# Pacing the gathers of GpSimd by their own landings: a graph attention and mixture-of-experts kernel

## Chip, cores and metric

The kernel runs on one core of one Trainium2 chip. The metric is device time in microseconds (us) of one execution; the median of the runs is compared. The profile comes from one further execution of the same program.

## The reference

3,125 nodes with 256 features and 50,000 edges, sorted by their target node. The input is normalised, a graph attention layer (8 heads of 32) and a second branch ("mix") are added to it, and then a layer of 8 weighted experts.

```python
xn = _layernorm(x, axis=-1)
# graph attention
h_prime = (xn @ W + b).reshape(n, K, F_OUT)
h_src = jnp.sum(h_prime * a_src, axis=2); h_trg = jnp.sum(h_prime * a_trg, axis=2)
e = leaky_relu(h_src[src] + h_trg[trg], 0.2)
exp_e = jnp.exp(e - jnp.max(e))
alpha = exp_e / (segment_sum(exp_e, trg)[trg] + 1e-10)
gnn = segment_sum(h_prime[src] * alpha[:, :, None], trg)
# mix: q, k, v of xn by a batch-normalised product, depthwise and grouped
# products, relu attention within a node, a residual product
x = x + gnn + mix(xn)
# experts: softmax weights w, two batch-normalised relu layers, output product
x = x + sum_e w[:, e] * (relu(bn(relu(bn(xn2 @ W1[e])) @ W2[e])) @ Wo[e] + bo[e])
```

## The kernel before

**Stages.** Up to about 67 us the nodes are projected, and a table `projected_rows` with 264 floats a node (256 projected features and 8 source scores) is written to device memory. Then come the edges, until about 670 us. The experts (feed-forward part) fill the rest.

**The edges.** They are cut into NG = 33 groups of EC = 12 chunks of 128 edges (the last group has 7 chunks). For a group `grp` these things are done, each engine running its own loop over the groups and all of them held together by semaphores:

- GpSimd, `gather(grp)` (L431 to L447): one indirect DMA for each chunk (L444) fetches the 128 rows of the sources from the table into `G[slot][:, c, :]`. There are SLOTS = 5 buffers G. It runs ahead of the other engines by LEAD = 2 groups.
- SyncE, `targets(g)` (L360): loads the targets of a group, spread over all partitions, into `dstb`, 384 KB, two buffers.
- VectorE, `window(g)`: makes a one-hot matrix `ohT` from `dstb` and the scores of the targets' window, `hsel`.
- TensorE, `targets(g)` (L757, raises `hte_ready`): twelve small matmuls of `ohT` and `hsel`, the target score of every edge.
- VectorE, `scores(g)` (L1175 on): waits for the gathers of g and for `hte_ready`, and adds source and target scores. ScalarE takes the exponentials (L489, L493).
- VectorE, `messages(g)`: a one-hot matrix `oh` (L1206), then the rows in G times the exponentials (L1218).
- TensorE, `sums(g)` (L768, raises `seg_ready`): twelve matmuls of `oh` and G, 128 x 264, which add the messages up by target.
- VectorE, `collect(g)` (L1224): adds the sums to the accumulator and raises `g_free` (L1257), so that the buffer G may be filled again.

**The mix branch** is woven into the same loops, one node tile (128 nodes, NT = 25) an iteration, t = g - 2: TensorE's `channels` (L803), `u_rows` (L814, three matmul pairs, each raising `u_mm`), `out_features` (L821) and `mixed_out` (L828, the residual product, raises `r_mm`); ScalarE's `squares` (L504, L506), `epsilon` and `mixed_out` (L527, which waits for `r_mm`); VectorE's `mix(t)` (L1320 to L1328).

**Order within an iteration g.** TensorE: targets(g+1), out_features, u_rows, early channels, sums(g), mixed_out, late channels. VectorE: messages(g), collect(g-1), scores(g+1), window(g+2), mix(g-2). ScalarE: out_features, exponentials(g+1), squares, epsilon, batch norm, mixed_out.

**What holds GpSimd.** At the head of group `grp` it waits for `g_free` of the group five back, and for `seg_ready` of grp - 2 (the sums of group grp - 3 are done). In front of the sixth gather (c == 5) it waits for `hte_ready` of grp, the target scores of group grp - 1, and in front of the tenth (c == 9) for `u_mm`, the matmuls of u_rows of the tile t = grp - 4. The twelve gathers of a group raise one semaphore, `gath[slot]`, by 16 each. None of these waits is for a gather itself.

`need(eng, sem, count)` waits if count is over zero.

Of the kernel before, what the change touches and what calls it, by code (L numbers as in the profile page):

```python
# [48 lines left out]
SLOTS = 5  # L49
# [5 lines left out]
LEAD = 2  # L55
# [47 lines left out]
def program(nc, a, out):  # L103
    with ExitStack() as ctx:
# [169 lines left out]
        ):  # L274
            s.update({k: sem(k) for k in names_.split()})
        x_part = [sem(f"x_part{i}") for i in range((NT - 1) // XT)]
        gath = [sem(f"gath{i}") for i in range(SLOTS)]
        dstl = [sem(f"dstl{i}") for i in range(2)]
        x_back = [sem(f"x_back{i}") for i in range(XS)]
        w_raw = [sem(f"w_raw{i}") for i in range(2)]  # L280
# [1 line left out]
        def exps(par, chunks=EC):  # L282

            return b_seg[par][:, EXPS:EXPS + chunks * H].rearrange("p (c h) -> p c h", c=chunks)

        def rounds_of(t):

# [125 lines left out]
        @block.gpsimd  # L413
        def _(pool):
            g = nc.gpsimd
            chain = Chain(pool, s["gchain"])
            g.memset(x_in[:, NT - 1, 0:F], 0.0).then_inc(s["x_pad"], 1)
            g.memset(src_l[:, NG - 1, :], 0).then_inc(s["edge_fill"], 1)
            g.memset(dst_l[:, NG - 1, :], PAD_DST).then_inc(s["edge_fill"], 1)
            g.memset(ones[:, :], 1.0).then_inc(s["consts"], 1)  # L420
            g.memset(ablk[:, :, :], 0.0).then_inc(s["consts"], 1)
            g.memset(ip[:, 1:MC + 1, :], 0.0).then_inc(s["consts"], 1)
            chain.link(g.memset(ident[:, :], 0.0))
            g.iota(row_i, pattern=[[1, P]], base=0, channel_multiplier=0).then_inc(s["consts"], 1)
            g.iota(col_i[:, :], pattern=[[0, 1]], base=0, channel_multiplier=1).then_inc(s["consts"], 1)
            g.affine_select(out=ident[:, :], in_=ident[:, :], compare_op=ALU.not_equal, fill=1.0, base=0,
                            pattern=[[-1, P]], channel_multiplier=1).then_inc(s["idn"], 1)
            g.memset(avg[:, :], 1.0 / P).then_inc(s["consts"], 1)
            g.memset(x_in[:, :, F:XP], 1.0).then_inc(s["consts"], 1)

            def gather(grp):  # L431
                slot, t = grp % SLOTS, grp - LEAD - MIX0
                need(pool, s["g_free"], grp - SLOTS + 1)
                if grp == 1:
                    pool.wait_ge(s["sw_mm"], 1)
                if grp == 2:
                    pool.wait_ge(s["var_mm"], 1)
                need(pool, s["seg_ready"], grp - LEAD)
                for c in range(CHUNKS[grp]):
                    if c == 5:  # L440
                        need(pool, s["hte_ready"], grp - LEAD + 2)
                    if c == 9 and 0 <= t < NT:
                        pool.wait_ge(s["u_mm"], 3 * t + 3)
                    g.indirect_dma_start(  # L444
                        out=G[slot][:, c, :], out_offset=None, in_=table[:, :],
                        in_offset=bass.IndirectOffsetOnAxis(ap=src_l[:, grp, c:c + 1], axis=0),
                    ).then_inc(gath[slot], 16)  # L447
            pool.wait_ge(s["edges"], 16 * 9)
            pool.wait_ge(s["tout"], 16 * NT)
            for grp in range(NG):  # L450
                gather(grp)

            pool.wait_ge(s["r_mm"], NT)
            g.memset(bo4, 0.0).then_inc(s["bo_clear"], 1)
# [528 lines left out]
        def _(dve):  # L983
# [185 lines left out]
            def scores(g):  # L1169

                ch, par = CHUNKS[g], g % 2
                z = zed[par][:, 0:ch, :]
                dve.wait_ge(gath[g % SLOTS], sum(16 * CHUNKS[i] for i in range(g % SLOTS, g + 1, SLOTS)))
                dve.wait_ge(s["hte_ready"], g + 1)
                V.tensor_reduce(z, parts_of(ch), AX.X, ALU.add).then_inc(s["z_part"], 1)  # L1175
                dve.wait_ge(s["z_part"], g + 1)
# [430 lines left out]
```

## Time and profile before

| | us |
|---|---|
| median of 3 runs | 1179.82 |
| lowest, highest | 1173.99, 1181.73 |
| the profiled execution, its own time | 1172.42 |
| its span (first to last instruction) | 1170.5 |
| TensorE busy | 964.0 |
| VectorE busy | 788.7 |
| ScalarE busy | 507.3 |
| GpSimd busy | 377.2 |

The span is divided by the last gathers: the edge groups' gathers run from 67.6 to 653.2 us, and what follows has none. The mean granted clock of TensorE is 0.91 of full speed. Busy time counts the instructions alone. A gather is 0.95 us of GpSimd's time, with 0.30 us to the next one; the transfer that it starts runs on the DMA engines afterwards. In a row of the order of time, the bracket at the end gives how long the engine sat idle in front of the instruction and who ended that; "issue" is time in which it waited for nothing that the profile shows, and "remote" a releaser that the profile cannot name.

### The profile page before, as it was taken

How to read it: one execution, taken by the hardware profiler on the slowest of the kernel's cores; microseconds unless marked ns; L12 is line 12 of the kernel's file. 1: busy time of each engine (PE TensorE's matmuls, PEld its weight loads, DVE VectorE, ACT ScalarE, POOL GpSimd, SP SyncE). 2: the span in 40 equal slices, each digit the busy share in tenths (PEclk: the TensorE clock that was granted, in tenths of full speed). 3: DMA queues.
4: the chain of work that ended last, by engine and by line, in shares of the span. 5: the costliest groups of instructions: out<-in, count | busy, mean ns of one | idle time of the engine just before them, and what ended most of it. 6: DMA issues, size and time to landing. Idle time of an engine off the chain costs nothing.

```text
span 1170.5 us, 14947 instructions
## 1 busy us (share of the span) xinstructions
PE 964.0 (82%) x5195; PEld 830.1 (71%) x5195; DVE 788.7 (67%) x1394; ACT 507.3 (43%) x1016; POOL 377.2 (32%) x408
## 2 busy tenths in 40 slices
PE   0998488878977788987763458999999999999996
PEld 0776376766866567776652347889978899998986
DVE  6786558878776788898865875666555554554544
ACT  1200044343442344444412135656645666666663
POOL 0034766666666666666666200000000000000000
PEclk9997788889988999898886677999999999999999
DMA  7332434443444444434455310000000000000012
GB/s 209 115 89 74 134 101 109 126 115 105 123 113 113 112 113 123 117 104 127 114 168 169 94 55 1 1 1 1 25 4 1 27 27 2 28 1 1 1 37 74
DMA packets 51371, 89.34 MB, mean 76 GB/s; under 512 B 10454, under 2 KB 34346, under 8 KB 51277
## 3 DMA queue, kind: packets, MB, share of 16 engines
q0 software_dynamic: 18768, 52.88, 16.8%
q1 hardware_dynamic: 32509, 35.27, 9.7%
q8 instruction: 52, 0.85, 0.3%
q14 instruction: 42, 0.34, 0.1%
HBM read 81.42 MB, written 6.68 MB: 75 GB/s over the span
## 4 chain that ended last, share of the span: by engine, by line
PE 47%; DVE 24%; another core or an unknown queue 9%; issue 9%; ACT 7%; DVEq 1%; DMA 1%; SPq 0%; ACTq 0%; POOL 0%; POOLq 0%
PE bank L888 12%; PE bank L889 11%; PE bank L890 11%; DVE U L1326 4%; DVE G L1218 4%; ACT junk L506 2%; PE bank L698 2%; PE bank L727 2%; DVE oh L1206 2%; DVE sums L1224 1%; PE bank L768 1%; PE bank L814 1%; PE bank L955 1%; DMA x_in<-in_x 1%
## 5 line engine op out<-in xcount | busy, mean ns | idle before, releaser
L444 POOL DMA_INDIRECT G<-projected_rows,src_l x391 | 373.8, 956 | 277.3 <-issue 108.1
L1489 DVE TENSOR_TENSOR hil<-hid,hil 128x1024 fp32r<-128x1024 f32 (+2 forms) x112 | 121.9, 1089 | 202.3 <-ACT hil L639 202.2
L768 PE MATMUL bank<-G,oh 128*128 128x264 f32 x782 | 194.8, 406 | 43.0 <-issue 23.7
L631 ACT ACTIVATE hid<-bank,faff 128x512 f32<-128x512 f32 (+2 forms) x224 | 158.8, 722 | 152.3 <-PE bank L890 150.2
L768 PEld LDWEIGHTS bank<-G,oh 128*128 128x128 f32 x782 | 155.5, 201 | 75.3 <-issue 27.3
L888 PE MATMUL bank<-ew,hil 128*128 128x256 f32 (+1 forms) x400 | 113.6, 284 | 1.5 <-DVE feat_rows L1501 1.5
L889 PE MATMUL bank<-ew,hil 128*128 128x256 f32 (+1 forms) x400 | 113.1, 283 | 0.0
L890 PE MATMUL bank<-ew,hil 128*128 128x256 f32 (+1 forms) x400 | 113.0, 282 | 0.0
L639 ACT CAST hil<-hid 128x1024 fp32r<-128x1024 f32 (+2 forms) x112 | 105.2, 940 | 9.8 <-ACT hid L631 0.4
L1218 DVE TENSOR_TENSOR G<-G,bank 128x3072 f32<-128x3072 f32 (+1 forms) x33 | 109.0, 3304 | 0.0
L803 PE MATMUL bank<-feat_rows,wqkv 128*128 128x256 f32 (+1 forms) x312 | 74.9, 380 | 24.0 <-ACT TT L521 17.2
L888 PE MATMUL bank<-frh,ew 128*128 128x512 f32 (+2 forms) x224 | 85.7, 383 | 9.9 <-DVE frl L1465 9.8
L1501 DVE SCALAR_TENSOR_TENSOR feat_rows<-bank,gate,feat_rows 128x256 f32<-128x256 f32 (+1 forms) x200 | 83.2, 475 | 5.7 <-PE bank L890 4.5
L1326 DVE RECIPROCAL U<-U 128x512 f32<-128x512 f32 x25 | 83.8, 3353 | 0.0
L889 PE MATMUL bank<-frl,ew 128*128 128x512 f32 (+2 forms) x224 | 83.7, 373 | 0.0
L890 PE MATMUL bank<-frh,ew 128*128 128x512 f32 (+2 forms) x224 | 83.5, 373 | 0.0
L803 PEld LDWEIGHTS bank<-feat_rows,wqkv 128*128 128x128 f32 x312 | 58.8, 194 | 34.8 <-ACT TT L521 19.5
L890 PE MATMUL bank<-hil,ew 128*128 128x512 f32 (+2 forms) x224 | 82.6, 369 | 0.0
L888 PE MATMUL bank<-hil,ew 128*128 128x512 f32 (+2 forms) x224 | 82.5, 368 | 0.0
L889 PE MATMUL bank<-hil,ew 128*128 128x512 f32 (+2 forms) x224 | 82.3, 367 | 0.0
L527 ACT COPY feat_rows<-bank 128x256 f32<-128x256 f32 x25 | 9.3, 372 | 168.2 <-remote 163.2
L888 PEld LDWEIGHTS bank<-ew,hil 128*128 128x128 f32 (+1 forms) x400 | 75.7, 189 | 3.1 <-issue 1.9
(292 smaller groups left out, 1686.8 us busy)
## 6 DMA issues: line engine op xcount, KB each, us to landing
dstb<-targets SPq DMA_DIRECT2D x32, 384.0 KB
G<-projected_rows,src_l POOLq DMA_INDIRECT x391
projected_rows<-sums SPq DMA_DIRECT2D x25, 132.0 KB, 3.2
x_in<-in_x SPq DMA_DIRECT2D x3, 1024.0 KB, 8.8
U<-in_x SPq DMA_DIRECT2D x24, 128.0 KB
out<-feat_rows SPq DMA_DIRECT2D x24, 128.0 KB
TT<-in_W SPq DMA_DIRECT2D x8, 256.0 KB
wqkv<-in_W SPq DMA_DIRECT2D x8, 256.0 KB
```

Source lines behind the costliest of these rows:

```text
L444: g.indirect_dma_start(out=G[slot][:, c, :], out_offset=None, in_=table[:, :], in_offset=bass.IndirectOffsetOnAxis(ap=src_l[:, grp, c:c + ...
L631: A.activation(hid[layer][:, m, 0:cols], bank[2 * layer + m][:, 0:cols], ACT.Relu, bias=faff[:, 2 * layer + 1, j:j + 1], scale=faff[:, 2 * ...
L639: A.copy(hidh[layer][par][:, :, 0:cols], hid[layer][:, :, 0:cols]).then_inc(hi, 1)
L768: ins = T.matmul(b_seg[g % 2][:, 0:ROW], oh[g % 2][:, c, :], G[g % SLOTS][:, c, :], start=(c == 0), stop=(c == ch - 1))
L803: ins = T.matmul(b_z[:, i * 256:i * 256 + cols], wqkv[:, k, c * P:(c + 1) * P], FM[:, k, start:start + cols], start=(k == 0), stop=(k == K ...
L888: T.matmul(out_, lh, rh, start=(k == 0), stop=False)
L889: T.matmul(out_, lh, rl, start=False, stop=False)
L890: return T.matmul(out_, ll, rh, start=False, stop=(k == KC - 1))
L1218: V.tensor_tensor(m3, m3, exps(par, ch)[:, :, :, None].broadcast_to([P, ch, H, DH]), ALU.mult).then_inc(s["msg_ready"], 1)
L1326: link(V.reciprocal(vbuf[par], vbuf[par]))
L1489: V.tensor_tensor(hidl[layer][par][:, :, 0:cols], hid[layer][:, :, 0:cols], hidh[layer][par][:, :, 0:cols].bitcast(F32), ALU.subtract).the ...
L1501: ins = V.scalar_tensor_tensor(out=m, in0=y.rearrange("p (c n) -> p c n", c=KC), scalar=gate[0:rows, t, e:e + 1], in1=m, op0=ALU.mult, op1 ...
```

## The change

GpSimd waits at the head of a group for `hte_ready` of the group (target scores of the one in front) and no longer for `seg_ready`; the wait in front of the sixth gather is gone. From the third gather of a group on, each waits until the one two back has landed. For that the gathers of even and of odd chunks raise separate semaphores, `gath[slot][0]` and `gath[slot][1]`, and `landed(grp, half)` is the value that one of them has when all of its gathers up to the group are in. The first two gathers of a group wait for no landing. VectorE waits for both semaphores ahead of its scores. The wait for `u_mm` in front of the tenth gather stays, and so does that for `g_free`.

```diff
-        gath = [sem(f"gath{i}") for i in range(SLOTS)]
+        gath = [[sem(f"gath{i}_{j}") for j in range(2)] for i in range(SLOTS)]
...
+        def landed(grp, half):
+
+            return 16 * sum((CHUNKS[i] + 1 - half) // 2 for i in range(grp % SLOTS, grp + 1, SLOTS))
...
-                need(pool, s["seg_ready"], grp - LEAD)
+                need(pool, s["hte_ready"], grp)
+                earlier = [landed(grp - SLOTS, half) for half in range(2)]
                 for c in range(CHUNKS[grp]):
-                    if c == 5:
-                        need(pool, s["hte_ready"], grp - LEAD + 2)
                     if c == 9 and 0 <= t < NT:
                         pool.wait_ge(s["u_mm"], 3 * t + 3)
+                    if c >= 2:
+                        pool.wait_ge(gath[slot][c % 2], earlier[c % 2] + 16 * (c // 2))
                     g.indirect_dma_start(
                         out=G[slot][:, c, :], out_offset=None, in_=table[:, :],
                         in_offset=bass.IndirectOffsetOnAxis(ap=src_l[:, grp, c:c + 1], axis=0),
-                    ).then_inc(gath[slot], 16)
+                    ).then_inc(gath[slot][c % 2], 16)
...
-                dve.wait_ge(gath[g % SLOTS], sum(16 * CHUNKS[i] for i in range(g % SLOTS, g + 1, SLOTS)))
+                for half in range(2):
+                    dve.wait_ge(gath[g % SLOTS][half], landed(g, half))
```

The order of instructions is the same on every engine; what moves is where GpSimd waits. Before, on GpSimd, one whole group (group 5, buffer G0) and the head of the next; a bracket names the semaphores that the instruction waits for:

```order
L444 DMA G0<-projected_rows,src_l 128x264 [waits seg_ready,g_free]
L444 DMA G0<-projected_rows,src_l 128x264 x4
L444 DMA G0<-projected_rows,src_l 128x264 [waits hte_ready]
L444 DMA G0<-projected_rows,src_l 128x264 x3
L444 DMA G0<-projected_rows,src_l 128x264 [waits u_mm]
L444 DMA G0<-projected_rows,src_l 128x264 x2
L444 DMA G1<-projected_rows,src_l 128x264 [waits seg_ready,g_free]
```

Now, on GpSimd, the last five gathers of the same group and the first three of the next (gath0_1 is the semaphore of buffer G0 and of the odd chunks):

```order
L449 DMA G0<-projected_rows,src_l 128x264 [waits gath0_1]
L449 DMA G0<-projected_rows,src_l 128x264 [waits gath0_0]
L449 DMA G0<-projected_rows,src_l 128x264 [waits gath0_1,u_mm]
L449 DMA G0<-projected_rows,src_l 128x264 [waits gath0_0]
L449 DMA G0<-projected_rows,src_l 128x264 [waits gath0_1]
L449 DMA G1<-projected_rows,src_l 128x264 [waits hte_ready,g_free]
L449 DMA G1<-projected_rows,src_l 128x264
L449 DMA G1<-projected_rows,src_l 128x264 [waits gath1_0]
```

Three stops in a group have become eleven: one at the head and ten for landings, one of which is also the one for u_mm.

## Rows read from the trace of the kernel before

**Rows 1.** Busy time of each engine over the span, from the page: us (share) xinstructions.

```profile
PE 964.0 (82%) x5195; PEld 830.1 (71%) x5195; DVE 788.7 (67%) x1394; ACT 507.3 (43%) x1016; POOL 377.2 (32%) x408
```

**Rows 2.** Busy time by stretch of the span; the first row is its columns.

```profile
core 0: us, PE busy (x) PEld busy (x) DVE busy (x) ACT busy (x) POOL busy (x), PEclk, DMA share, GB/s
...
129.50:344.90 215.40, 167.00 (x818) 140.20 (x817) 160.61 (x207) 78.49 (x211) 137.72 (x144) 0.88 0.41 114
...
653.20:1170.50 517.30, 481.44 (x2844) 431.75 (x2844) 295.47 (x563) 295.77 (x426) 1.89 (x2) 0.95 0.06 19
```

**Rows 3.** Order of time, 319.5 to 329 us: start, duration, engine, line, operation [idle before <-releaser].

```profile
319.31 0.83 PE L768 MATMUL bank<-G,oh 128*128 128x264 f32 x3
...
321.70 0.45 PE L757 MATMUL bank<-hsel,ohT 128*128 128x24 bf16 x12
...
323.83 0.95 POOL L444 DMA_INDIRECT G<-projected_rows,src_l  x1 [0.30 <-issue]
327.14 0.37 ACT L527 COPY feat_rows<-bank 128x256 f32<-128x256 f32 x1 [10.11 <-remote]
...
327.77 0.95 POOL L444 DMA_INDIRECT G<-projected_rows,src_l  x1 [2.99 <-remote]
```

**Rows 4.** Order of time, 340 to 346 us, the end of the next group.

```profile
339.72 1.05 PE L768 MATMUL bank<-G,oh 128*128 128x264 f32 x4
...
341.55 0.95 POOL L444 DMA_INDIRECT G<-projected_rows,src_l  x1 [0.30 <-issue]
...
344.75 0.43 PE L757 MATMUL bank<-hsel,ohT 128*128 128x24 bf16 x11 [0.50 <-issue]
...
345.60 0.94 POOL L444 DMA_INDIRECT G<-projected_rows,src_l  x1 [3.11 <-DVEq L1257]
```

**Rows 5.** Order of time of GpSimd alone, 111 to 594 us: starts of groups 3, 4 and 29.

```profile
111.58 0.95 POOL L444 DMA_INDIRECT G<-projected_rows,src_l  x1 [0.30 <-issue]
...
129.53 0.95 POOL L444 DMA_INDIRECT G<-projected_rows,src_l  x1 [0.30 <-issue]
...
148.72 0.94 POOL L444 DMA_INDIRECT G<-projected_rows,src_l  x1 [4.50 <-remote]
...
593.41 0.94 POOL L444 DMA_INDIRECT G<-projected_rows,src_l  x1 [2.83 <-DVEq L1257]
```

**Rows 6.** Who waited for whom, 160 to 650 us: us in total, times, longest.

```profile
ACT feat_rows L527 <- remote: 163.2, 21, 16.5
...
POOL G L444 <- remote: 43.2, 18, 3.8
...
PE bank L821 <- ACT feat_rows L527: 24.9, 16, 5.5
```

**Rows 7.** Order of time, 331 to 333 us and 359 to 370.2 us: starts within a stream.

```profile
332.20 0.60 ACT L504 ACTIVATE U<-bank 128x512 f32<-128x512 f32 x1 [1.02 <-PE bank L814]
...
362.00 0.94 POOL L444 DMA_INDIRECT G<-projected_rows,src_l  x1 [1.42 <-remote]
...
369.89 0.59 ACT L497 COPY oT<-bank 128x512 f32<-128x512 f32 x1 [5.36 <-remote]
...
370.07 0.94 POOL L444 DMA_INDIRECT G<-projected_rows,src_l  x1 [2.13 <-remote]
```

**Rows 8.** Busy time by stretch behind the last gather of group 1; columns as in rows 2.

```profile
113.40:113.80 0.40, 0.40 (x2) 0.30 (x3) 0.00 (x0) 0.00 (x0) 0.00 (x0) 0.50 0.59 190
113.80:114.10 0.30, 0.30 (x2) 0.29 (x1) 0.00 (x0) 0.00 (x0) 0.00 (x0) 0.50 0.09 28
```

**Rows 9.** Busy time by stretch around the load of targets of one group, same columns.

```profile
312.80:314.20 1.40, 1.40 (x8) 1.22 (x7) 0.76 (x3) 1.40 (x5) 1.09 (x2) 1.00 0.81 229
...
315.60:317.00 1.40, 1.40 (x8) 1.21 (x7) 1.40 (x2) 1.40 (x3) 1.09 (x2) 1.00 0.47 124
```

**Rows 10.** Order of time of VectorE, 306 to 327.5 us: the messages of two groups.

```profile
306.32 3.35 DVE L1218 TENSOR_TENSOR G<-G,bank 128x3072 f32<-128x3072 f32 x1
...
322.70 3.35 DVE L1218 TENSOR_TENSOR G<-G,bank 128x3072 f32<-128x3072 f32 x1
```

## The prediction

> **What bounds the kernel now.** I read the engine lines of the page first. TensorE is busy 82% of the span, VectorE 67%, GpSimd 32% [rows 1]; by that alone a change to GpSimd would be worth nothing. So the second look is the table of stretches [rows 2]: from 653 us on GpSimd has ended (1.9 us in 517) and the change cannot reach that half. From 129.5 to 344.9 us, twelve of the edge groups, TensorE is busy 167.0 of 215.4 us (78%), VectorE 160.6 (75%) and GpSimd 137.7 (64%), and none is full. Something in their handshake sets the pace.
>
> The third view is the order of time around one group's end [rows 3]. GpSimd issues the last gather of group 13 at 323.83 us and then sits until 327.77 (2.99 us, for "remote", which is the profile's word for a releaser it cannot name). It waits for seg_ready of group 11, and that is the TensorE run at L768 that ended at 320.14 us. The target scores (L757) ended at 322.15; the residual product, for which ACT L527 waits, stands between the two in TensorE's order. Yet the consumers start together much later: ACT L527 at 327.14 after 10.11 us idle, GpSimd at 327.77. So TensorE's signals are seen 5 to 7 us after they were due, and only when the stream of gathers has stopped: the last one began at 323.83. The next group's end is the same: sums done 340.77, last gather 341.55, GpSimd at 345.60 after 3.11 [rows 4]. Group start to group start is 17.83 us, of which 15.0 are gathers and 2.8 this wait. Over the stretch: 129.53 to 593.41 us, 26 groups from 3 to 28, 17.84 us each [rows 5]. In the list of waits that is ACT L527 with 163.2 us in 21 waits, and GpSimd with 43.2 in 18 under "remote" alone [rows 6]. The wait at the head of a group is thus partly GpSimd's own doing: it waits for a signal that appears to come through when its own gathers are quiet.
>
> Are signals ever on time within a stream? Yes. ACT L504 starts at 332.20, 4.4 us into a burst, behind a matmul of L814 that the view names with a wait of 1.02 us; at 362.00 GpSimd itself goes on after only 1.42 us idle [rows 7]. At 370.07, in front of the sixth gather, the rest came through after a stop of 2.13 us. Short pauses do let some through. How long a pause is needed the trace does not say, and the forecast hangs on that.
>
> **The change, part by part.** (1) *A gather waits for the one two back.* What one needs from start to landing: the last gather of group 1 starts at 111.58 us [rows 5], and the DMA engines still move 190 GB/s from 113.4 to 113.8 and nearly nothing (28 GB/s) from 113.8 to 114.1 [rows 8]. That is between 2.2 and 2.5 us; I take 2.4. From a signal to the first instruction behind it I allow 0.3: ACT and GpSimd start at 369.89 and 370.07 on one release [rows 7]. So a pair of gathers takes 2.7 us where it took 2.50. The last two of a group start a pair of 2.50 themselves, so 12 gathers occupy 5 x 2.7 + 2.5 = 16.0 us instead of 15.0. Lower bound 15.0 (the landing is hidden wholly), upper 5 x 2.9 + 2.5 = 17.0.
>
> The Trainium skill, "DMA: Bandwidth & Descriptors", Anatomy of one DMA, gives a software-issued transfer about 2.0 us plus its bytes over 436 GB/s, so 2.31 us for 128 x 264 floats. By that an estimated pair is hardly over 2.50 and the pacing is free, which would leave 12 gathers at 15.0 us; the rows above allow it only at their lowest edge. The case that this would lead to stands among the rivals.
>
> (2) *Slow landings.* Once a group a load of 384 KB of targets runs beside the gathers, and 229 GB/s are moved from 312.8 to 314.2 us against 124 a little later, with the engines' share up from 0.47 to 0.81 [rows 9]. A gather in that stretch lands later. Before, nothing waited for it; now the gather two behind does. Bounds: 0, and 1.6 (the length of a stretch and a little more). I take 1.1, near the upper one, since the share is near full. Should two waits in a row be hit, up to 2.5.
>
> (3) *The second wait in front of the tenth gather*, u_mm beside the landing: no row has two waits in mid-stream. Bounds 0 and 0.7 us; the idle in front of a group's first gather, which has two, lies 0.63 us behind ACT's start on the same release (327.77 against 327.14 [rows 3]), and one wait in mid-stream only 0.18 (370.07 against 369.89 [rows 7]). Taken 0.2, since it runs beside the landing.
>
> (4) *The head waits for target scores instead of sums, and the wait in front of the sixth gather goes.* That sixth wait was mostly free; it cost 2.13 us in group 16 and similar in few others. The head's new signal is L757, 2.0 us later than L768 in the one group (322.15 against 320.14 [rows 3]) and 4.4 us later in the next (345.18 against 340.77 [rows 4]). GpSimd's start at 345.60 lies 0.4 us behind the later of them already, so as long as both are held it costs 0.2 us or so. If they are seen on time, L757 is done 12.2 us (322.15 less 309.96, which is 327.77 less the period) or 17.4 us (345.18 less 327.77) into the group in front. The second figure would bind, but it is itself late by TensorE's waits for ACT L527, 24.9 us in 16 and up to 5.5 each [rows 6], and ACT L527 waits for a held signal too. I cost this part at nothing, cover: the gathers themselves. Queued behind GpSimd's waits are gathers only; VectorE's scores wait for them a group ahead.
>
> (5) VectorE waits on two semaphores where one was: under 0.1 us, beside the 16.4 us that its own iteration takes (L1218 at 306.32 and at 322.70 [rows 10]).
>
> Sum for a group with signals that come through in the short pauses: 16.0 + 1.1 + 0.2 = 17.3 us, over VectorE's 16.4, which is next. Against 17.84 that is 0.54 less, times 26 groups 14.0 us. Groups 0 to 2 and 29 to 32 I leave as they are (bounds -6 and +5: the run of 24 gathers that ends some 4.5 us before 148.72 is now cut at 129.53, where a stop of some 4 us lets TensorE's signals out earlier; the 4.50 us stop at 148.72 [rows 5] shows what is there). 1172.42 less 14.0 is 1158.4. The median of the runs shown is 7.4 over the profiled execution, so 1165.8: I say 1166.
>
> **Rivals.**
> *The hold stays (slower).* The pauses that pacing makes are 0.2 us a pair, far shorter than the 1.42 and 2.13 us [rows 7] that let signals through, and there is always a gather in flight until the last has landed. Then the head is released as before, some 4.0 us after the last gather's start (323.83 to 327.77, 341.55 to 345.60), plus 0.2 for the later signal. The last start moves from 13.75 to 14.75 us, or 16.05 with the slow landings. The period is 18.95 to 20.25 us, 1.1 to 2.4 above today's, times 26: +29 to +63 us, in the middle +46: 1226. For it: the two group ends, where the signals came out only with the stream's end [rows 3, 4]. Against it: those that were seen within a stream [rows 7]. It decides early: a held head costs 1.1 to 2.4, a free one saves 0.54, so between a fifth and a third of the heads held eats the gain. Chance 0.30.
>
> *Halfway.* Some heads are held and some not, or the slow landings cost 2.0 us a group: period about 18.2, +0.35 x 26 = +9, so 1189, between 1172 and 1205. For it: the mixed picture from 359 to 371 us [rows 7]. Chance 0.21.
>
> *The hold goes and the landings hide (faster).* With 15.0 to 16.2 us of gathers VectorE's 16.4 sets the pace: 1.44 x 26 = 37 us less, 1142. For it: few landings may be slow once GpSimd never has three under way. Against: the 2.2 to 2.5 us and the load beside them are there in any case. Chance 0.11.
>
> *The forecast* (signals come through, 17.3 us a group). For it: a signal 4.4 us into a burst, with two gathers under way, was seen at once [rows 7], and the pacing never lets the number rise over two, nor lets the engines' queue grow behind a slow landing. Against it: the same two are under way at a group's end, where the signals were held [rows 3]. Chance 0.38, own range 1150 to 1180.
>
> **How the numbers follow.** A measurement tells about 1% from no change, 12 us, so faster is under 1168 and slower over 1192. The forecast's case gives 0.24 to faster, 0.13 to same and 0.01 to slower; the fast rival 0.11 to faster; halfway 0.10 to same and 0.11 to slower; the hold 0.30 to slower. Together 0.35, 0.23, 0.42. The single likeliest time is still 1166, although more of the chance lies above it than below. The range runs from 1141, the fast rival, to 1232, which takes in the middle of the hold's span; beyond stay about 0.1 on each side.
>
> **What would show it.** Idle of about 0.5 us (the 0.3 of before in it) in front of every second gather, put down to its landing, and 16 to 17.5 us from a group's first gather to the end of its last; ACT L527's 163.2 us should fall under 60; the wait at a group's head should shrink from 3 us to under 1. If instead ACT L527 keeps 7 us and the head 3 us, the hold has stayed and I am wrong by +46. If the gathers' stretch is over 18 us, part (2) was too low. The part from 653 us on should be as long as now, 517 us; if it moves by over 5 us the reasoning by groups doesn't cover it.

## The result, and the profile after

The changed kernel takes 1227.63 us (median of 4 runs, 1222.92 to 1237.57) against 1178.39 us for the kernel before on the same chip: ratio 1.0444, 95% interval 1.0395 to 1.0492. It is slower by 49 us; 1166 was predicted. The profiled execution took 1225.46 us, its span is 1223.7.

The page of the changed kernel, the chain of work that ended last and GpSimd's group of gathers:

```profile
PE 43%; DMA 24%; issue 12%; DVE 12%; ACT 4%; POOL 4%; DVEq 0%; SPq 0%; ACTq 0%; POOLq 0%
...
L449 POOL DMA_INDIRECT G<-projected_rows,src_l x391 | 376.4, 963 | 343.5 <-DMA G<-projected_rows,src_l 201.3
```

A quarter of the span now hangs on landings of DMAs, nearly all of them of gathers; in the chain of the kernel before all landings together are 1%. In the waits of the changed kernel, 160 to 720 us (us in total, times, longest), the answer to [rows 6] is:

```profile
POOL G L449 <- DMA G<-projected_rows,src_l: 172.9, 203, 3.9
...
ACT oT L502 <- PE bank L826: 47.9, 16, 4.9
...
POOL G L449 <- PE bank L819: 15.9, 14, 1.6
...
ACT feat_rows L532 <- PE bank L833: 3.5, 1, 3.5
```

ScalarE's wait for the residual product, L532 now and L527 before, has fallen from 163.2 us for "remote" to 3.5 us, and no wait for "remote" stands in the list. The delay of TensorE's signals, which I call the hold from here on, is gone. And yet the kernel is slower. Where that comes from is in the order of time of GpSimd alone, one whole group (group 13) of the changed kernel:

```profile
332.17 0.94 POOL L449 DMA_INDIRECT G<-projected_rows,src_l  x1 [0.30 <-issue]
333.42 0.95 POOL L449 DMA_INDIRECT G<-projected_rows,src_l  x1 [0.30 <-issue]
335.18 0.95 POOL L449 DMA_INDIRECT G<-projected_rows,src_l  x1 [0.81 <-DMA G<-projected_rows,src_l]
336.50 1.21 POOL L449 DMA_INDIRECT G<-projected_rows,src_l  x1 [0.38 <-issue]
338.78 0.95 POOL L449 DMA_INDIRECT G<-projected_rows,src_l  x1 [1.07 <-DMA G<-projected_rows,src_l]
340.03 0.95 POOL L449 DMA_INDIRECT G<-projected_rows,src_l  x1 [0.30 <-issue]
341.84 0.95 POOL L449 DMA_INDIRECT G<-projected_rows,src_l  x1 [0.85 <-DMA G<-projected_rows,src_l]
343.10 0.95 POOL L449 DMA_INDIRECT G<-projected_rows,src_l  x1 [0.32 <-DMA G<-projected_rows,src_l]
344.87 0.95 POOL L449 DMA_INDIRECT G<-projected_rows,src_l  x1 [0.83 <-DMA G<-projected_rows,src_l]
346.85 0.95 POOL L449 DMA_INDIRECT G<-projected_rows,src_l  x1 [1.03 <-DMA G<-projected_rows,src_l]
348.11 0.94 POOL L449 DMA_INDIRECT G<-projected_rows,src_l  x1 [0.31 <-issue]
349.85 0.95 POOL L449 DMA_INDIRECT G<-projected_rows,src_l  x1 [0.79 <-DMA G<-projected_rows,src_l]
351.10 0.95 POOL L449 DMA_INDIRECT G<-projected_rows,src_l  x1 [0.31 <-issue]
```

The head of the next group, 351.10, comes 1.25 us behind the last gather: the head waits for nothing any more, here and in the other groups from 3 to 28 (1.27 at most). But from a gather to the one two behind it go 3.01 us (332.17 to 335.18), 3.06 (338.78 to 341.84), 3.03 (341.84 to 344.87), where it was 2.50. From the third to the fifth gather go 3.60 (335.18 to 338.78), and from the eighth to the tenth 3.75 (343.10 to 346.85).

All groups together, GpSimd's first gathers of groups 3 and 29 in the changed kernel, the answer to [rows 5]:

```profile
135.18 0.95 POOL L449 DMA_INDIRECT G<-projected_rows,src_l  x1 [0.30 <-issue]
...
646.81 0.95 POOL L449 DMA_INDIRECT G<-projected_rows,src_l  x1 [0.30 <-issue]
```

That is 511.6 us for 26 groups, 19.68 each, against 17.84. The span grew by 53.2 us: 5.6 ahead of group 3 (135.18 against 129.53), 47.8 in the 26 groups, and in sum nothing behind (576.9 us from group 29 to the end against 577.1). That nothing is made of two parts. The last gathers start at

```profile
721.96 0.95 POOL L449 DMA_INDIRECT G<-projected_rows,src_l  x1 [2.46 <-DMA G<-projected_rows,src_l]
```

now and at 653.18 before, so groups 29 to 32 take 15.4 us longer (75.15 against 59.77), and what follows the last gather takes 15.6 us less, 501.7 against 517.3. Most of the 15.6 is the work on groups that are already gathered: the last matmuls of `sums` start 13 us behind the last gather now (735.2) and 25 us before (678.4), since a GpSimd that sets the pace has no lead any more. From there to the end it is 488.5 against 492.1 us. So the loss is GpSimd's own pace, and the other engines follow it. The stretch that stands in [rows 2] is this in the changed kernel:

```profile
129.50:344.90 215.40, 154.03 (x755) 127.09 (x754) 143.52 (x187) 71.33 (x194) 126.58 (x133) 0.88 0.37 104
```

Every engine is busy less, TensorE 154 us for 167, VectorE 144 for 161, and the DMA engines move 104 GB/s for 114.

### The profile page after: what moved, and what is told of

It reads as the page before. It is cut to its first block, busy times and chain, and to the rows that moved or that the text cites. A ratio compares the mean times of both kernels' runs of the same rounds, so it can differ in the third digit from the quotient of the medians.

```text
span 1223.7 us, 14974 instructions
## 1 busy us (share of the span) xinstructions
PE 969.0 (79%) x5195; PEld 832.3 (68%) x5195; DVE 790.0 (65%) x1394; ACT 505.9 (41%) x1016; POOL 379.8 (31%) x408
## 4 chain that ended last, share of the span: by engine, by line
PE 43%; DMA 24%; issue 12%; DVE 12%; ACT 4%; POOL 4%; DVEq 0%; SPq 0%; ACTq 0%; POOLq 0%
DMA G<-projected_rows,src_l 23%; PE bank L893 11%; PE bank L895 11%; PE bank L894 11%; POOL G L449 3%; DVE U L1332 3%; PE bank L703 2%; PE bank L732 2%; ACT junk L511 1%; PE bank L960 1%; DMA x_in<-in_x 1%; PE bank L819 1%; PE bank L826 1%; PE bank L773 1%; DVE bank L1333 1%
## 5 line engine op out<-in xcount | busy, mean ns | idle before, releaser
L494 ACT ACTIVATE G<-zed,negc 128x96 f32<-128x96 f32 (+1 forms) x33 | 12.3, 374 | 288.1 <-issue 182.7
L808 PE MATMUL bank<-feat_rows,wqkv 128*128 128x256 f32 (+1 forms) x312 | 80.4, 405 | 37.4 <-ACT TT_odd L526 16.8
L826 PE MATMUL bank<-ip,U 128*128 128x128 f32 x100 | 23.3, 376 | 94.2 <-DVE U L1334 90.9
L808 PEld LDWEIGHTS bank<-feat_rows,wqkv 128*128 128x128 f32 x312 | 61.5, 206 | 51.9 <-ACT TT_odd L526 19.2
L1181 DVE TENSOR_REDUCE zed<-bank 128x96 f32<-128x288 f32 (+1 forms) x33 | 15.0, 454 | 121.9 <-issue 106.1
L893 PE MATMUL bank<-frh,ew 128*128 128x512 f32 (+2 forms) x224 | 84.4, 377 | 9.9 <-DVE frl L1471 9.8
L893 PE MATMUL bank<-hil,ew 128*128 128x512 f32 (+2 forms) x224 | 82.5, 368 | 0.0
L895 PE MATMUL bank<-hil,ew 128*128 128x512 f32 (+2 forms) x224 | 82.1, 366 | 0.0
L895 PE MATMUL bank<-frh,ew 128*128 128x512 f32 (+2 forms) x224 | 82.1, 366 | 0.0
```

What stands on the lines that cost most here:

```text
L808: ins = T.matmul(b_z[:, i * 256:i * 256 + cols], wqkv[:, k, c * P:(c + 1) * P], FM[:, k, start:start + cols], start=(k == 0), stop=(k == K ...
L893: T.matmul(out_, lh, rh, start=(k == 0), stop=False)
L895: return T.matmul(out_, ll, rh, start=False, stop=(k == KC - 1))
```

## The experiments

Three theories are tested. A: the landing waits do everything, the loss of time and the end of the hold. B: the head's new wait ended the hold. C, formed after the first four runs: whether signals are held depends on the chip; its rival D stands beside it below. No chip is known to have been met on two occasions, so where the text says "a chip with the hold", a passing condition of that occasion is not excluded. All ratios are to the kernel before, timed on the same chip beside the kernel.

**The halves of the change.** Head alone:

```diff
-                need(pool, s["seg_ready"], grp - LEAD)
+                need(pool, s["hte_ready"], grp)
                 for c in range(CHUNKS[grp]):
-                    if c == 5:
-                        need(pool, s["hte_ready"], grp - LEAD + 2)
```

> Half of the change alone: the head of a group waits for hte_ready, the wait in front of the sixth gather is gone, no gather waits for a landing. Theory A (the landing waits did it all, both the time and the end of the hold): the stream is unbroken as before, so TensorE's signals stay held; GpSimd stops some 3 us at each head, the period is 17.8 to 18.1 us and the time 1178 to 1190. Theory B (the head's wait is what ended the hold): GpSimd goes from group to group with under 1 us idle, ACT L527 has no waits of 7 us, and VectorE's 16.4 us set the period: 1140 to 1155.

Measured: 1117.49 us, ratio 1.0001 (0.999 to 1.0013). That looked like theory B, but the kernel before took 1118.32 us on this chip, not 1178. The half alone changed nothing; what had changed is the chip or the occasion. Landing waits alone (the changed kernel with these two waits put back):

> The other half alone: the landing waits, with the head on seg_ready and the wait in front of the sixth gather on hte_ready as before. Theory A: nothing but the landings is waited for, the period is 19.6 to 19.8 us as in the changed kernel and the time 1222 to 1232, with no hold. Theory B: the hold is back, the head costs 3 to 4 us on top, 1270 or more.

Measured: 1234.07 us, ratio 1.104 (1.1017 to 1.1063). All of the loss comes from the landing waits, as theory A has it; what ended the hold this pair can't show, since the kernel before had none here.

**The kernel before and after on such a chip.**

> The kernel before, unchanged, for a profile beside the kernels sent with it. In the last comparison it took 1118 us where it takes 1178 in the runs shown, and the halves sent with it showed no signal held. Theory C (whether TensorE's signals are held is a property of the chip or its day and not of the kernel): a time near 1118 comes with a period of 16.2 us, ACT L527 without long waits and heads of about 1 us; a time near 1178 comes with 17.8 us, ACT L527 at 160 us or so and heads of 3 us. Theory D (something else differs, say the memory or the clock): the two times come with the same waits, and all stages are longer in proportion.

> The changed kernel, unchanged. Theory C: its gathers are paced by their landings alone, 19.6 to 19.8 us a group on any chip, since none of its signals were held in its first profile either: 1222 to 1232, a ratio of 1.044 where the kernel before has its signals held and 1.095 to 1.10 where it has not. Theory D: it is shorter by the same 5% as the kernel before, 1165, ratio 1.044.

Measured, on another chip: 1117.81 us for the kernel before (ratio 1.0000) and 1234.06 for the changed one, ratio 1.1016 (1.097 to 1.1062). That is theory C's numbers within 2 us, and D falls: the changed kernel takes 1228 to 1234 on both kinds of chip, the kernel before does not. The waits of the kernel before on this chip, 160 to 620 us:

```profile
POOL G L444 <- PE bank L768: 31.5, 15, 4.7
ACT feat_rows L527 <- PE bank L828: 30.6, 23, 6.7
```

No releaser is "remote" in that list, and ScalarE starts as soon as TensorE is done. Order of time there, around one group's end:

```profile
263.73 0.39 PE L768 MATMUL bank<-G,oh 128*128 128x264 f32 x1
263.89 0.95 POOL L444 DMA_INDIRECT G<-projected_rows,src_l  x1 [0.30 <-issue]
263.95 1.89 PE L828 MATMUL bank<-wres,oT 128*128 128x256 f32 x8
265.15 0.95 POOL L444 DMA_INDIRECT G<-projected_rows,src_l  x1 [0.30 <-issue]
265.88 0.37 ACT L527 COPY feat_rows<-bank 128x256 f32<-128x256 f32 x1 [0.16 <-PE bank L828]
266.40 0.95 POOL L444 DMA_INDIRECT G<-projected_rows,src_l  x1 [0.31 <-issue]
```

The same stream of gathers 1.25 us apart, in the same kernel, and in the middle of it ScalarE starts 0.04 us behind the end of the residual product (263.95 + 1.89 against 265.88); in [rows 3] it took until the stream had ended.

"Remote" can be looked into further, for the traces keep the time of every semaphore update. Between 160 and 600 us of the kernel before with the hold, 71 of TensorE's 188 updates are stamped over 1 us behind the end of their matmuls, and 45 of the 71 lie 2.9 to 3.6 us behind the start of a group's last gather. In the trace without the hold it is none of 207, in the changed kernel of the first chip none of 165. VectorE's and ScalarE's updates are in time in all three.

The first gathers of groups 3 and 29 stand at 128.63 and 548.43 us in the trace without the hold, so 16.15 us a group.

```profile
548.43 0.94 POOL L444 DMA_INDIRECT G<-projected_rows,src_l  x1 [2.32 <-PE bank L768]
```

What bounds it there is the loop of VectorE, with its wait for ScalarE's squares (L506): between 300 and 360 us the chain of work that ended last has no gather among its larger parts.

```profile
by line: DVE U L1326 22.4%; DVE G L1218 21.8%; issue 16.7%; ACT junk L506 11.4%; DVE sums L1224 5.4%; DVE bank L1327 4.7%; DVE U L1323 3.5%; DVE ksum L1322 3.0%; DVE zed L1175 2.5%; DVE oh L1206 2.2%; ACT bank L493 2.2%; DVE zed L1202 1.9%;
```

The spans of the two profiled executions of the kernel before differ by 54.0 us: 44.1 in the 26 groups (1.7 each), 9 behind them, of which 7 are the work on gathered groups, and 1 ahead; the part behind the last `sums` is the same (492.1 and 491.8). The medians differ by 60.

**The head alone on a chip with the hold.** The kernel of the first experiment again; this time the kernel before took 1176.66 us.

> The head's new wait alone, a second time, for a chip on which the kernel before takes 1178 if one is met: theory A there (only the landing waits ended the hold) 1178 to 1190, theory B 1140 or less. On a chip where it takes 1117: 1117 again.

Measured: 1176.95 us, ratio 0.9995 (0.9973 to 1.0018). Theory B is out: with the new head and no landing waits the hold is there in full. The landing waits are thus needed for its end. Whether they end it without the new head was not seen, for that kernel met only a chip without the hold. Its order of time around one head:

```profile
328.22 0.45 PE L755 MATMUL bank<-hsel,ohT 128*128 128x24 bf16 x12
...
330.88 0.95 POOL L442 DMA_INDIRECT G<-projected_rows,src_l  x1 [0.30 <-issue]
334.17 0.37 ACT L525 COPY feat_rows<-bank 128x256 f32<-128x256 f32 x1 [10.61 <-remote]
...
335.02 0.94 POOL L442 DMA_INDIRECT G<-projected_rows,src_l  x1 [3.19 <-DVEq L1255]
```

This is the picture of [rows 3] again: target scores done at 328.67, the consumers start from 3.3 us behind the last gather's start on, GpSimd at 335.02.

**What a landing costs.** One back in place of two:

```diff
-                    if c >= 2:
-                        pool.wait_ge(gath[slot][c % 2], earlier[c % 2] + 16 * (c // 2))
+                    if c >= 1:
+                        pool.wait_ge(gath[slot][(c - 1) % 2], earlier[(c - 1) % 2] + 16 * ((c + 1) // 2))
```

> The changed kernel with a wait for the gather just in front in place of the one two back. If a landing as seen by GpSimd's next gather is 3.02 us whatever the number under way, 12 gathers take 11 x 3.02 + 1.25 = 34.5 us, with slow landings 35 to 36.5: (35.5 - 16.15) x 31 = 600 over the 1117 of the kernel before, 1700 to 1740. If most of the 0.6 us between the end of a transfer and the next gather comes from having two under way, it is 2.7 a gather, 31 us a group, 1580.

Measured: 1762.13 us, ratio 1.4976. GpSimd in one group of it, in order of time:

```profile
501.86 0.95 POOL L449 DMA_INDIRECT G<-projected_rows,src_l  x1 [0.30 <-issue]
504.92 0.94 POOL L449 DMA_INDIRECT G<-projected_rows,src_l  x1 [2.11 <-DMA G<-projected_rows,src_l]
508.52 0.95 POOL L449 DMA_INDIRECT G<-projected_rows,src_l  x1 [2.66 <-DMA G<-projected_rows,src_l]
511.53 0.94 POOL L449 DMA_INDIRECT G<-projected_rows,src_l  x1 [2.06 <-DMA G<-projected_rows,src_l]
514.71 0.95 POOL L449 DMA_INDIRECT G<-projected_rows,src_l  x1 [2.24 <-DMA G<-projected_rows,src_l]
```

It is 3.06, 3.60, 3.01 and 3.18 us from one gather to the next, with no other gather under way; the 3.60 has a load of targets beside it, issued at 504.56. So the 3.0 is what a gather takes alone, not contention of two. A group takes 36.42 us here (174.69 to 1121.61 for 26), in place of the 35.5 that the expected 1700 to 1740 was built on. Between 511.53 and 514.71 the stretches show the DMA engines' share (second-last column; the one in front is the granted clock):

```profile
512.00:513.00 1.00, 1.00 (x4) 0.73 (x4) 0.96 (x2) 0.00 (x0) 0.47 (x1) 0.50 0.00 0
513.00:513.40 0.40, 0.40 (x2) 0.32 (x1) 0.40 (x1) 0.00 (x0) 0.00 (x0) 0.50 0.61 127
513.40:514.00 0.60, 0.60 (x7) 0.32 (x6) 0.57 (x2) 0.00 (x0) 0.00 (x0) 0.58 0.41 141
```

Data move between 1.5 and 2.5 us behind the gather's start, and the next gather starts 0.7 us later still. The time in between has two parts, and this trace tells them apart, for here the profile can match the gathers with their semaphores:

```profile
DMA to landing us min/median/max: 2.7/2.8/6.0
```

The semaphore is raised 2.78 us behind the gather's start in the median, 0.3 us behind the end of the traffic (2.44 us), and the gather that waits for it starts 0.26 us behind that: 3.04 us together. The 0.3 that I had allowed for the start on a signal was right. What I had taken for the landing, the end of the traffic, comes 0.3 us before it.

The Trainium skill, "DMA: Bandwidth & Descriptors", Anatomy of one DMA, gives about 2.0 us plus the bytes over 436 GB/s for a DMA that GpSimd issues, an estimate of 2.31 us for this one. The landing measured here is 2.8 us, and the measurement decides. By that estimate and the 0.26 us a pair would have taken 2.57 us, and the two-back wait would have been nearly free.

Without the loads of targets:

```diff
             def targets(g):
                 edges = CHUNKS[g] * P
-                need(sp, s["dstb_free"], g - 1)
+                if g > 1:
+                    return
...
-                dve.wait_ge(dstl[par], 16 * (g // 2 + 1))
+                dve.wait_ge(dstl[par], 16)
```

> The changed kernel without the loads of targets (384 KB a group) after the first two groups. Left out: those loads, so that the target scores of the later groups come from old targets; SyncE does not wait for dstb_free either. Theory: the third and fourth gather of a group now wait up to 1 us more than the others because they or those behind them land beside that load. Then 12 gathers take 5 x 3.02 + 2.5 = 17.6 us, plus 0.5 for u_mm in front of the tenth, so 18.1 in place of 19.7: about 1180 to 1190. Rival: landings are slow from the gathers themselves or from other traffic, and 19.2 to 19.7 stays: 1215 to 1230.

Measured, on a chip with the hold: 1212.11 us, ratio 1.0301 (1.0261 to 1.0341), between theory and rival. Its first gathers of groups 3 and 29 in the order of time:

```profile
135.18 0.95 POOL L450 DMA_INDIRECT G<-projected_rows,src_l  x1 [0.30 <-issue]
...
633.09 0.95 POOL L450 DMA_INDIRECT G<-projected_rows,src_l  x1 [0.30 <-issue]
```

19.15 us a group, where the changed kernel has 19.68 in the first comparison and 19.75 in its second. The loads cost 0.5 us a group, not 1.1. They hit one gather: from the third to the fifth go 4.07 us in the mean of groups 3 to 28 with them and 3.30 without. This run is also the second with landing waits on a chip with the hold, and the hold is gone in it too: no wait for "remote", and 2 of TensorE's 180 updates over 1 us late.

Without the wait for `u_mm` in front of the tenth gather (its two lines taken out of the changed kernel):

> The changed kernel without the wait for u_mm in front of the tenth gather, which then waits for its landing alone. The tenth gather now starts 1.95 us behind the ninth where other odd ones take 1.35 to 1.65, so if a second wait costs its own step, 0.4 to 0.5 us a group for 25 groups go: 1214 to 1219. If it is u_mm itself that is late there (TensorE's L819 ends 14 waits, 15.9 us), the gathers gain up to 16 us in all: 1211. If the wait costs nothing, 1227.

Measured: 1216.59 us, ratio 1.0907 (1.0865 to 1.0949), against 1.1016 with it on another chip without the hold. 1.1% of 1117 is 12 us, 0.5 us for each of 25 groups, as expected. The traces show it directly: in the changed kernel without the hold the tenth gather starts 0.74 us behind the landing of the eighth, in nearly every group, where gathers with one wait start 0.26 us behind theirs.

**How deep the cap.** Three back (a semaphore for each c % 3; the counts in `landed` and `earlier` and VectorE's waits follow) and four back, likewise with four:

```diff
-        gath = [[sem(f"gath{i}_{j}") for j in range(2)] for i in range(SLOTS)]
+        gath = [[sem(f"gath{i}_{j}") for j in range(3)] for i in range(SLOTS)]
...
-                    if c >= 2:
-                        pool.wait_ge(gath[slot][c % 2], earlier[c % 2] + 16 * (c // 2))
+                    if c >= 3:
+                        pool.wait_ge(gath[slot][c % 3], earlier[c % 3] + 16 * (c // 3))
```

> The changed kernel with a wait for the gather three back (three semaphores a buffer) in place of two. Theory A1 (a turnaround of 2.45 us landing plus 0.6 us wake-up sets the pace, and any cap on gathers under way ends the hold): 3.05 us now stand against three issues of 1.25 = 3.75, so only slow landings and the tenth gather's two waits cost anything; 15.5 to 16.5 us of gathers a group, VectorE's 16.4 to 17.0 set the period, 1145 to 1160. Theory A2 (the hold ends only where two are the cap, that is where gathers pause): signals are held, ACT L527 waits 7 us and more, heads 3 us: 1178 to 1195.

> A wait for the gather four back (four semaphores a buffer). 3.05 us of turnaround stand against 5.0 us of issues, and even a landing of 3.9 us is hidden, so the gathers take 15.1 to 15.4 us a group and VectorE's 16.2 sets the period. Without held signals: ratio 0.998 to 1.003. It also prices the ten further waits a group by themselves: if a satisfied wait costs 0.1 us each, the gathers take 16 us and still nothing is lost.

Measured on chips without the hold: three back 1125.55 us, ratio 1.0067 (1.0042 to 1.0091), and again 1123.06, ratio 1.0051 (1.0035 to 1.0066); four back 1117.04, ratio 1.0002 (0.9983 to 1.002). The first of these expected 1145 or more and came out lower, as its chip had no hold and VectorE's loop is 16.15 us and not 16.4 or more. The order of the times follows from the 3.0 us: a wait two back sets them against two issues of 1.25, so it always binds; three back against 3.75, so only slow landings bind; four back against 5.0, which hides nearly all of these too. The eight waits a group of four back, nearly all already met, cost next to nothing: from the first to the twelfth gather go 13.94 us with them and 13.84 without (means of groups 3 to 28). On the second of these chips three back had this on record:

> A wait for the gather three back, a second time. Where signals are not held in the kernel before: 1.007 as measured. Where they are held there: with a cap of three they are either held here too (1178 to 1195, ratio about 1.00 to 1.01), or not (1123 to 1130, ratio 0.955).

Both kernels and two others were timed on one more chip.

> A wait for the gather three back, for a chip on which signals are held. Theory cap (three under way and never a fourth is enough): signals on time, VectorE's 16.2 to 16.4 us a group, 1120 to 1130 where the kernel before takes 1177, ratio 0.955. Theory pauses (GpSimd must stop for about half a microsecond every other gather): the gathers run at 1.25 us most of the time, so the hold stays: 17.8 to 18.5 us a group, ratio 1.00 to 1.02. Where the kernel before takes 1117: 1.005 again.

> Four back. Theory cap: four under way hardly occur in the kernel before either, so the hold is the same as there, ratio 0.995 to 1.005. Theory pauses: the same. If this one too is free of the hold where three back is, it is the wait instruction itself between two gathers that ends it. Where the kernel before takes 1117: 1.000.

> Three back without the wait for u_mm in front of the tenth gather. On a chip without held signals VectorE's 16.2 sets the period, and the gathers' 16.2 shrink to 15.8: ratio 1.000 to 1.003 instead of 1.005 to 1.007. On a chip with them: as h1, or 0.5 less.

The kernel before took 1117.71 us there. Three back: 1126.91, ratio 1.008 (1.0055 to 1.0105); four back: 1118.91, ratio 1.0004 (0.9985 to 1.0022); three back without u_mm: 1123.06, ratio 1.0053 (1.0036 to 1.007), where 1.000 to 1.003 was expected, so the wait for u_mm is not the larger part of what three back costs. They say nothing on the hold. Three back was timed on one chip more:

> Three back once more. If the kernel before takes about 1177 here: theory cap 1120 to 1130 (ratio 0.955), theory pauses 1177 to 1200 (ratio 1.00 to 1.02). If it takes 1117: 1.005 to 1.008, and nothing new.

1123.93 us, ratio 1.0067 (1.0049 to 1.0084), the kernel before 1117.74: no hold there either. Whether three back ends the hold wasn't seen.

**Pauses only at the end of a group**, `if c >= 8` in place of `if c >= 2` in the changed kernel:

> The changed kernel with the two-back wait only from the ninth gather on (c >= 8), four waits a group. The gathers take 15.0 + two turnarounds (1.1) + 0.5 for the tenth = 16.6 us. Theory pauses or cap: both say that signals due near the end of a group are seen on time; 16.6 to 17.2 us a group, 1130 to 1150 on a held chip, ratio 0.965 to 0.975. Rival (what has once been held is let out only by a dry stream): the last four pauses don't free what was raised before, ratio 1.00 to 1.03. Where the kernel before takes 1117: 16.6 against 16.2, ratio 1.01.

> Two back from the ninth gather on, once more. If the kernel before takes about 1177 here: 1142 to 1150 (ratio 0.97 to 0.975) if pauses where the signals fall due are enough, 1180 to 1215 if only a dry stream lets out what was held. If it takes 1117: 1.022 again.

Measured: 1142.43 us, ratio 1.0225 (1.0208 to 1.0242), and 1141.38, ratio 1.0224 (1.0204 to 1.0243), both without the hold. Expected was 1.01 for the first of them. GpSimd's waits over the whole span in that one:

```profile
POOL G L449 <- DMA G<-projected_rows,src_l: 97.1, 122, 4.3
```

With these 122 waits, four a group, the kernel takes 25 us more, and a group takes 16.81 us: each wait that truly waits adds its part, wherever it stands, as soon as GpSimd's group is longer than VectorE's 16.2 us.

**One dry moment a group** in the kernel before:

```diff
+                full = sum(16 * CHUNKS[i] for i in range(slot, grp, SLOTS))
                 for c in range(CHUNKS[grp]):
+                    if c == 6:
+                        pool.wait_ge(gath[slot], full + 16 * c)
```

> The kernel before with one landing wait a group: the seventh gather waits until the sixth has landed, so that the stream runs dry once in the middle. A drained stop costs 3.02 - 1.25 = 1.8 us, so 12 gathers take 16.9 us. Where TensorE's signals are not held in the kernel before (1117), that is 0.7 over VectorE's 16.2 a group: +15 to +22, ratio 1.013 to 1.02. Where they are held (1178): if one dry moment lets them out, the period falls to some 17.0 and the time to 1145 to 1160; if not, it rises to 19 and 1210.

Measured, with the hold: 1191.69 us, ratio 1.0123 (1.0094 to 1.0152). One group of its gathers in the order of time, with the stop:

```profile
281.38 0.94 POOL L447 DMA_INDIRECT G<-projected_rows,src_l  x1 [2.69 <-remote]
...
287.62 0.94 POOL L447 DMA_INDIRECT G<-projected_rows,src_l  x1 [0.30 <-issue]
290.62 0.94 POOL L447 DMA_INDIRECT G<-projected_rows,src_l  x1 [2.06 <-DMA G<-projected_rows,src_l]
291.87 0.95 POOL L447 DMA_INDIRECT G<-projected_rows,src_l  x1 [0.30 <-PE bank L771]
```

And in its waits, 160 to 620 us:

```profile
ACT oT L500 <- remote: 55.1, 11, 9.8
...
ACT feat_rows L530 <- remote: 32.5, 8, 6.3
```

The dry stream costs 3.00 us for 1.25 in this group (287.62 to 290.62) and 3.72 in the mean of groups 3 to 28. ACT L530 waits 32.5 us for "remote" instead of 163.2, so some signals come out there. But others are held: new waits for "remote" take their place, and 103 of TensorE's 184 updates between 160 and 600 us are over 1 us late. The measured time lies between the two cases that were expected, and is no gain.

## Why the prediction was wrong

The forecast was 14 us faster, from 17.3 us a group; 19.68 were measured, and 49 us slower. The measured 1227.63 us lies inside the range of 1141 to 1232, but that reached so far up only for the rival in which the hold stays. By its steps:

- *Which case came.* The forecast's condition, that the signals come through, was met: no "remote" waits, heads of 1.25 us, ACT L532 at 3.5 us. The rival that gives nearly the measured number, the hold that stays with 1226, is not what happened: it had 3 to 4 us at each head and ScalarE's waits unchanged. The agreement in the number is chance, and the traces tell them apart. I gave slower 0.42 in all, but only 0.01 of it to the case that came.
- *Part (1), the turnaround, is the step that failed.* I took the end of the traffic, 2.4 us, for the landing, and 0.3 us from signal to next gather, 2.7 a pair. 3.0 is measured, with two under way and with one. The traffic ends at 2.4 us and the start on the signal takes 0.26; but the semaphore is raised only at 2.8 us, and no row that I had showed a landing. The basis of the 0.3, two engines that start 0.18 us apart on one release, gave no time from a signal to a start either, so that it came out right is luck. So 12 gathers take 5 x 3.02 + 2.5 = 17.6 us by my own sum, not 16.0, and my upper bound of 17.0 for this term was below what it is. Alone this turns the sign: 17.6 with my other terms is 18.9.
- *Part (2), the loads.* Taken 1.1 us, measured 0.5 (the run without them). My sign "over 18 us, part (2) was too low" pointed at the wrong term: the stretch is 19.4 us in the mean, and part (2) was too high.
- *Part (3), the second wait of the tenth gather.* Taken 0.2, measured 0.5 (the run without it), inside its bounds.
- *What the terms leave.* 17.6 + 0.5 + 0.5 is 18.6; 19.68 is measured. Where the other 1.1 us stands, the mean starts of groups 3 to 28 in the changed kernel show. The odd-numbered gathers follow each other after 3.22, 4.07, 3.04, 3.04 and 3.40 us, and the last two starts take 1.65 and 1.25, in sum 19.67. So the landings of the first and third gather are slow beyond the loads (3.31 and 3.30 us in the run without these), and the last pair takes 2.90 and not the 2.50 of my sum, because the twelfth gather waits for the tenth, which u_mm's wait made late. What makes the first landings of a group slow stays open; the one-back kernel, too, takes about 2 us a group more than 34.5.
- *Part (4), the head's wait.* At nothing, right: 1.0001 and 0.9995, on both kinds of chip. On a chip with the hold that run's groups take 18.30 us (132.48 to 608.32), and no trace of the kernel before on that chip stands beside it.
- *Part (5) and VectorE's floor.* Near: 16.15 to 16.24 us a group wherever neither hold nor pacing binds, where I had 16.4.
- *Outside 26 groups.* Bounds were -6 and +5: it was +5.6 ahead of group 3 and in sum nothing behind. But I had said that the part behind the last gather would stay within 5 us of 517, and it is 15.6 shorter: the sum by groups left out that GpSimd's lead at the end is work still to be done, and that it vanishes when GpSimd sets the pace.
- *The range of the case.* My own upper bounds summed to 17.0 + 2.5 + 0.7 = 20.2 us a group, some 1240 us. I gave the case 1150 to 1180 around the taken values, which is narrower than its terms allowed.

Why did a freed stream lose nevertheless? The kernel before is limited by the hold on chips that have it (17.84 us a group) and by VectorE on those that haven't (16.15). The two-back wait sets a third limit of 19.7 that lies above both. What it gains, the end of the hold, is worth at most 1.7 us a group, and it costs 4.7 us in the gathers (19.7 against 15.0), for which the stop of 2.8 us at the head was the only slack.

*What stays open:* what in the pacing ends the hold, the cap of two or the pauses; whether a cap of three, which costs 0.5 to 0.8% without the hold, ends it too, in which case it would gain some 4% where the hold is (an estimate: 1125 against 1177 us); and what lies behind the two kinds, the chip itself or something of the occasion. The three-back, four-back and last-four kernels met only chips without it. No kernel of this study was faster than the kernel before on its chip.

## What to carry to other kernels

To cap transfers under way, first take the whole turnaround from one issue to the issue that waits for it, not the end of the traffic, and divide: with 3.0 us and issues of 1.25 us a wait two back always binds, three back at times (0.5 to 0.8%), four back without a measurable cost. Waits that are already met cost next to nothing here, so a depth with room for slow landings gives the cap without the pace. Whether such a cap still ends a hold was not seen. And an engine's slack in front of a late signal is no slack if the wait for it goes: compare the new pace with the next limit behind (here VectorE's 16.2), not with the period of before.

## What the runs showed of the hardware

- The kernel before takes 1176.7 to 1178.4 us on two occasions and 1117.2 to 1118.3 on four, these on four different chips, with all runs of an occasion within 0.8%. The difference stands in the edge groups (17.84 against 16.15 us a group) and in one thing, that TensorE's semaphore updates come late while gathers stream (71 of 188 over 1 us late against none of 207): ACT L527 waited 163.2 us for "remote" on the one kind and 30.6 us for TensorE itself on the other.
- On chips with that delay the landing waits two back, together with the new head, remove it (two traces), and so does a wait one back. One dry stop a group moves it: ACT's wait for the residual product falls to 32.5 us, other waits grow.
- A gather of 128 rows of 264 floats ends its traffic 2.4 us behind its start and raises its semaphore at 2.8 us; a gather that waits for it starts 0.26 us later, 3.0 us in all, alone or with another beside it. With a second wait in front, for another semaphore, it starts 0.74 us behind the landing.
